# The causal convolution of a Mamba block taken into the input projection: four products per half on shifted columns

## The reference

```python
h = relu(adj @ layernorm(x) @ gcn_w + gcn_b)
h = (h - mean) * rsqrt(var + eps) * ln_g + ln_b
xz = h @ w_in                        # 128 -> 512
xc, z = xz[:, :256], xz[:, 256:]
xpad = pad(xc, 3 zero rows in front)
xconv = sum(xpad[k:k + L] * conv_w[:, k] for k in range(4)) + conv_b
u = silu(xconv)
dbc = u @ w_xp                       # 8 columns for dt, 16 for B, 16 for C
dt = softplus(dbc[:, :8] @ w_dt + b_dt)
# scan over tokens, 256 channels x 16 states:
#   state = exp(dt * A) * state + dt * B * u ;  ys = state . C
y = (ys + u * D) * silu(z)
x = x + y @ w_out
# then a mixture of 8 experts on layernorm(x): H = gelu(x @ W1 + b1), 128 -> 512,
# logits, argmax, x = x + prob * (H @ Wd[e] + bd[e])
```

## Time and profile before

| | us |
|---|---|
| median of 3 runs | 1770.6 |
| lowest, highest | 1767.5, 1779.21 |
| profiled execution, its own time | 1772.06 |
| its span (first to last instruction) | 1770.3 |
| DVE, PE, ACT, POOL busy | 1539.9, 1436.2, 883.5, 882.9 |
| mean granted TensorE clock | 0.921 |

### The profile page before, as it was taken

The page is one execution under the profiler, slowest core; times in us unless marked ns, Lnnn a source line. Parts: engine busy times, 40 slices in busy tenths (PEclk is TensorE's granted clock), DMA queues, the critical chain, the costliest instruction groups (busy, mean ns, idle before and its releaser), DMA issues. The chain is left out here.

```text
span 1770.3 us, 15687 instructions
## 1 busy us (share of the span) xinstructions
PE 1436.2 (81%) x4051; PEld 657.9 (37%) x4051; DVE 1539.9 (87%) x2038; ACT 883.5 (50%) x1574; POOL 882.9 (50%) x466
## 2 busy tenths in 40 slices
PE   6988998888888979898898888898889983522586
PEld 2433343333333434343444434343434441211343
DVE  8056989999999999999999999999999999999631
ACT  3143445453637465654747383646556473834421
POOL 0013334535346455655656564656566565656741
PEclk9999999999999999999999999999999996656698
DMA  8878999999998878788787978787887975334240
GB/s 304 279 287 274 339 343 336 348 364 354 359 331 292 299 285 304 288 292 316 266 323 263 311 266 282 278 302 276 284 318 280 324 245 171 114 115 141 86 124 12
DMA packets 151278, 476.90 MB, mean 269 GB/s; under 512 B 19694, under 2 KB 33058, under 8 KB 151060
## 3 DMA queue, kind: packets, MB, share of 16 engines
q1 hardware_dynamic: 104308, 315.57, 50.1%
q10 hardware_dynamic: 38560, 139.48, 22.9%
q0 software_dynamic: 8320, 20.86, 3.5%
HBM read 445.75 MB, written 32.97 MB: 270 GB/s over the span
## 5 line engine op out<-in xcount | busy, mean ns | idle before, releaser
L1210 PE MATMUL ps_adj<-ring,nodes 128*128 128x512 f32 x2048 | 954.4, 612 | 100.0 <-DMA ring<-adj 58.4
L499 POOL TENSOR_TENSOR h_c<-hidden,bc_ring 128x1024 f32<-128x1024 f32 x256 | 601.2, 2349 | 790.2 <-DVE inject L1070 534.6
L997 DVE TENSOR_TENSOR_SCAN hidden<-decay,state,inject 128x512 f32<-128x512 f32 x512 | 627.4, 1267 | 46.7 <-ACT decay L594 23.8
L1210 PEld LDWEIGHTS ps_adj<-ring,nodes 128*128 128x128 f32 x2048 | 389.7, 196 | 618.6 <-issue 454.2
L594 ACT ACTIVATE decay<-dt_sb,negA 128x512 f32<-128x512 f32 x512 | 339.4, 712 | 9.2 <-DVE dt_sb L1024 7.1
L1070 DVE TENSOR_TENSOR inject<-dtu_sb,bc_ring 128x1024 f32<-128x1024 f32 x256 | 314.1, 1227 | 14.5 <-DMA bc_ring<-bc_dram 12.7
L587 ACT COPY state<-hidden 128x2 f32<-128x2 f32 x255 | 49.1, 193 | 518.8 <-DVE hidden L997 518.4
L1040 DVE TENSOR_TENSOR y_sum<-y_sum,h_c 128x1024 f32<-128x1024 f32 x224 | 273.5, 1221 | 26.8 <-POOL h_c L499 23.4
L463 POOL DMA_INDIRECT out<-o_sb,out_at x68 | 100.0, 1471 | 55.7 <-DVE o_sb L900 42.5
L458 POOL DMA_INDIRECT bins<-rec,dest x60 | 87.3, 1455 | 10.8 <-issue 10.2
L453 POOL DMA_INDIRECT got<-bins,row_at x60 | 85.3, 1421 | 14.6 <-issue 11.6
(11 more groups left out here) (209 smaller groups left out, 1289.9 us busy)
## 6 DMA issues: line engine op xcount, KB each, us to landing
ring<-adj SPq DMA_DIRECT2D x512, 512.0 KB, 5.7
bc_ring<-bc_dram ACTq DMA_DIRECT2D x256, 512.0 KB, 6.4
wd_ring<-wd_rows SPq DMA_DIRECT2D x64, 288.0 KB, 5.2
bins<-nodes SPq DMA_DIRECT2D x32, 516.0 KB, 8.4
nodes<-x_rows ACTq DMA_DIRECT2D x8, 512.0 KB, 12.0
x_tile<-x_rows SPq DMA_DIRECT2D x16, 256.0 KB, 7.9
wd_rows<-Wd SPq DMA_DIRECT2D x8, 256.0 KB, 7.8
ring<-Wd SPq DMA_DIRECT2D x1, 2048.0 KB, 7.4
```

Source lines behind the costliest of these rows:

```text
L499: nc.gpsimd.tensor_tensor(h_c[:, s % 2], hidden[:, s % 2], over_halves(bc_ring[:, s % BC_RING, 1]), ALU.mult).then_inc(hc_ready, 1)
L997: scan = nc.vector.tensor_tensor_scan(hidden[:, s % 2, h], decay[:, s % 2, h], inject[:, h], state[:, h, s:s + 1], ALU.mult, ALU.add)
L1210: last = nc.tensor.matmul(ps_adj[:, 0], nodes[:, m], ring[:, g % RING, m % GROUP], start=(m == 0), stop=(m == J - 1))
```

## The change

The convolution is linear, so it goes into the projection. For each half h and tap k there is a weight win_taps[k, h] = w_in (half h) x ln_g x conv_w[:, k] (per output column). The normalised tile goes to a new buffer `hn_sb` with the last three columns of the tile before in front, and PE adds four products, each on hn_sb shifted by k columns, into one bank per half. ACT then makes u = SiLU(bank + bias) in one instruction per half. `conv_in`, the first tap on ACT and the three taps on DVE are gone. z's products now come first (f[5]) and are evicted in f[6]; the taps of half 0 stand in f[6], those of half 1 in f[7]. The fourth W1 product of the FFN moves from slot 7 to slot 8, behind the product for dbc, and the order of the GELUs follows. The counts of adjacency groups in the slots change (`SHARE`, for i from 4 on, and `MAIN[-1]`).

New at the start: the rows of conv_w are spread over the partitions by a product of the mean matrix (1/128 everywhere) with eight diagonals (times 128), on PE in the middle of tile 0's adjacency product (`tap_rows`), and multiplied with w_in and ln_g by DVE. The bias has four columns per half: in the very first tile the first three tokens see fewer taps, so they have their own (three one-column SiLUs per half in body -1).

```diff
-SHARE = (3, 3, 2, 3, 2, 2, 2, 1, 2, 2, 0, 3, 2, 3, 0, 2)
-MAIN = {-2: EVEN, -1: (0, 1, 1, 0, 0, 1, 0, 0, 5, 1, 0, 1, 1, 1, 1, 0),
+SHARE = (3, 3, 2, 3, 3, 2, 1, 0, 2, 2, 2, 3, 2, 3, 0, 1)
+MAIN = {-2: EVEN, -1: (0, 1, 1, 0, 0, 1, 0, 0, 1, 1, 0, 2, 2, 2, 2, 0),
...
-        conv_in = sb("conv_in", [P, 2, TAPS - 1 + T])
+        hn_sb = sb("hn_sb", [P, TAPS - 1 + T])
...
+        win_raw = H[:, 1].rearrange("p (k c) -> p k c", k=4)
+        diagonals = H[:, 2:4]
...
                     if front and s == f[3]:
+                        if i >= 0:
+                            c.wait(xz_done, 1, 0)
+                            nc.scalar.copy(hn_sb[:, 0:TAPS - 1], hn_sb[:, T:]).then_inc(tail_ready, 1)
                         c.wait(var_done, 1, 1)
...
                     if front and s == f[6]:
-                        c.wait(conv_step, 1, 0)
-                        nc.scalar.copy(conv_in[:, :, 0:TAPS - 1], conv_in[:, :, T:T + TAPS - 1]
-                                       ).then_inc(tail_ready, 1)
-                        c.wait(tail_ready, 1, 1)
+                        c.wait(y_ready, -1, 1)
                         for h in range(2):
                             c.wait(xz_done, 1, h + 1)
-                            nc.scalar.activation(conv_in[:, h, TAPS - 1:], ps_f[:, h], ACT.Identity,
-                                                 bias=xz_bias[:, h:h + 1]).then_inc(xz_ready, 1)
-                    if front and s == f[7]:
-
-                        c.wait(y_step, 0, 1)
-                        for h in range(2):
-                            c.wait(xz_ready, 1, h + 1)
-                            nc.scalar.activation(u_sb[:, h], conv_in[:, h, 0:T], ACT.Identity,
-                                                 bias=vec("conv_b", h), scale=vec("conv_w", TAPS * h)
-                                                 ).then_inc(conv_first, 1)
-                    if front and s == f[7]:
-                        c.wait(y_ready, -1, 1)
-                        for h in range(2):
-                            c.wait(xz_done, 1, h + 3)
                             nc.scalar.activation(z_sb[:, q, h], ps_f[:, h], ACT.Identity,
                                                  bias=xz_bias[:, h + 2:h + 3]).then_inc(xz_ready, 1)
...
                     if front and s == f[8]:
-                        c.wait(conv_step, 1, 2 * (TAPS - 1))
-                        nc.scalar.activation(u_sb[:], u_sb[:], ACT.Silu).then_inc(u_ready, 1)
-                        c.wait(xz_ready, 1, 4)
+                        c.wait(y_step, 0, 1)
+                        for h in range(2):
+                            c.wait(xz_done, 1, 3 + h)
+                            if i == -1:
+                                for t in range(TAPS - 1):
+                                    nc.scalar.activation(u_sb[:, h, t:t + 1], ps_f[:, h, t:t + 1], ACT.Silu,
+                                                         bias=tap_bias[:, h, t:t + 1])
+                            first = TAPS - 1 if i == -1 else 0
+                            silu = nc.scalar.activation(u_sb[:, h, first:], ps_f[:, h, first:], ACT.Silu,
+                                                        bias=tap_bias[:, h, TAPS - 1:TAPS])
+                        silu.then_inc(u_ready, 1)
+                        c.wait(xz_ready, 1, 2)
                         nc.scalar.activation(z_sb[:, q], z_sb[:, q], ACT.Silu)
...
-                        for k in (3, 0, 1, 2):
+                        for k in range(4):
...
+            nc.vector.tensor_scalar_mul(win_z[:], win_raw[:, 2:4], vec("ln_g")).then_inc(start_v, 1)
+            for h in range(2):
+                for k in range(TAPS):
+                    diag = nc.vector.tensor_scalar(diagonals[:, h, k * P:(k + 1) * P], ident, vec("conv_w", TAPS * h + k),
+                                                   float(P), ALU.mult, ALU.mult)
...
+            dve.wait_ge(taps_done, 1)
+            for h in range(2):
+                nc.vector.scalar_tensor_tensor(
+                    out=win_taps[:, :, h], in0=win_raw[:, h].unsqueeze(1).broadcast_to([P, TAPS, P]),
+                    scalar=vec("ln_g"), in1=ps_e[:, h].rearrange("p (k c) -> p k c", k=TAPS),
+                    op0=ALU.mult, op1=ALU.mult).then_inc(taps_ready, 1)
...
                         c.wait(rstd_ready, 1, 1)
-                        nc.vector.tensor_tensor(front_a[:], ps_f[:, 0], front_b[:], ALU.mult).then_inc(hn_ready, 1)
+                        c.wait(tail_ready, 1, 0)
+                        nc.vector.tensor_tensor(hn_sb[:, TAPS - 1:], ps_f[:, 0], front_b[:], ALU.mult
+                                                ).then_inc(hn_ready, 1)
...
-                    if front and s == f[7]:
-
-                        for k in range(1, TAPS):
-                            for h in range(2):
...
-                                nc.vector.scalar_tensor_tensor(
-                                    out=u_sb[:, h], in0=conv_in[:, h, k:k + T], scalar=vec("conv_w", TAPS * h + k),
-                                    in1=u_sb[:, h], op0=ALU.mult, op1=ALU.add).then_inc(conv_step, 1)
...
+            def tap_rows():
+
+                pe.wait_ge(diag_ready, 1)
+                for h in range(2):
+                    last = product(ps_e[:, h], [(mean, diagonals[:, h])])
+                last.then_inc(taps_done, 1)
...
+                        if (tile, g) == (0, 3 * GROUPS // 4):
+                            tap_rows()
...
                     if front and s == f[5]:
                         c.wait(hn_ready, 1, 1)
-                        for k in range(2):
-                            product(ps_f[:, k], [(win_sb[:, k], front_a[:])]).then_inc(xz_done, 1)
-                    if front and s == f[6]:
-                        for k in range(2):
-                            c.wait(xz_ready, 1, k + 1)
-                            product(ps_f[:, k], [(win_sb[:, 2 + k], front_a[:])]).then_inc(xz_done, 1)
+                        for h in range(2):
+                            product(ps_f[:, h], [(win_z[:, h], hn_sb[:, TAPS - 1:])]).then_inc(xz_done, 1)
+                    if front and s in f[6:8]:
+                        h = f[6:8].index(s)
+                        c.wait(xz_ready, 1, h + 1)
+                        product(ps_f[:, h], [(win_taps[:, k, h], hn_sb[:, k:k + T]) for k in range(TAPS)]
+                                ).then_inc(xz_done, 1)
                     if ffn and s == 7:
...
-                        for k in range(4):
-                            if k == 3:
-                                c.wait(xz_ready, 1 if front else 0, 4 if front else 0)
+                        for k in range(3):
                             product(h_bank(k), [(w1_sb[:, k], xn_cols)]).then_inc(h_done, 1)
...
+                    if ffn and s == 8:
+                        product(h_bank(3), [(w1_sb[:, 3], xn_cols)]).then_inc(h_done, 1)
                     if front and s == f[9]:
                         c.wait(low_ready, 1, 1)
                         if ffn:
-                            c.wait(h_ready, -1, 1)
+                            c.wait(h_ready, -1, 4)
```

More of the change, by code:

```diff
@@ L75, in gnn_mamba_moe @@
         gcn_sb = sb("gcn_sb", [P, P])
-        win_sb = sb("win_sb", [P, 4, P])
+        win_z = sb("win_z", [P, 2, P])
+        win_taps = sb("win_taps", [P, TAPS, 2, P])
         w1_sb = sb("w1_sb", [P, 4, P])
@@ L84, in gnn_mamba_moe @@
         xz_bias = sb("xz_bias", [P, 4])
+        tap_bias = sb("tap_bias", [P, 2, TAPS])
         eps_col = sb("eps_col", [P, 1])
@@ L348, in small_weights @@
                 sp.wait_ge(pad_ready, 1)
-                for dst, src in ((vec_sb[:], vecs), (const_sb[:], consts), (gcn_sb[:], gcn_w), (win_sb[:], w_in),
+                for dst, src in ((vec_sb[:], vecs), (const_sb[:], consts), (gcn_sb[:], gcn_w), (H[:, 1], w_in.rearrange("p k c -> p (k c)")),
                                  (wxp_sb[:], w_xp), (wdt_sb[:], w_dt[0:40]), (wout_sb[:], w_out), (w1_sb[:], W1), (wg_sb[:, :, 0:EXPERTS], Wg),
@@ L789, in _ @@
             nc.vector.memset(state[:], 0.0).then_inc(start_v, 1)
-            nc.vector.memset(conv_in[:], 0.0).then_inc(start_v, 1)
+            nc.vector.memset(hn_sb[:, 0:TAPS - 1], 0.0).then_inc(start_v, 1)
             nc.vector.memset(eps_col[:], EPS).then_inc(start_v, 1)
@@ L823, in _ @@
             dve.wait_ge(start_p, 1)
-            nc.vector.tensor_scalar_mul(win_sb[:], win_sb[:], vec("ln_g")).then_inc(start_v, 1)
+            nc.vector.tensor_scalar_mul(win_z[:], win_raw[:, 2:4], vec("ln_g")).then_inc(start_v, 1)
[3 more added lines that the diff above has]
+                                                   float(P), ALU.mult, ALU.mult)
+            diag.then_inc(diag_ready, 1)
+            dve.wait_ge(start_a, 2)
+            taps = vec("conv_w", 0, 2 * TAPS).rearrange("p (h k) -> p h k", h=2)
+            for n in range(TAPS):
+                so_far = tap_bias[:, :, n - 1] if n else vec("conv_b", 0, 2)
```

(12 more changed lines are left out.)

9 lines of the change are left out of this document (3 added, 6 removed).

## The result

| | before | after |
|---|---|---|
| median, us | 1774.8 (4 runs) | 1794.4 (4 runs) |
| lowest to highest | 1767.5 to 1779.2 | 1791.3 to 1804.6 |
| profiled execution, own time | 1772.06 | 1804.58 |
| its span | 1770.3 | 1802.8 |
| mean granted clock | 0.921 | 0.930 |

The ratio is 1.0116, interval 1.0062 to 1.017: slower by 1.2%, where 1738 (0.982 of the median then shown) was forecast.

The account below looks back on a forecast made before the run. It took DVE, 96% busy in the middle, as the bound, PE next. Eleven middle bodies gave -31 us and the start -1: 1772.06 became 1740, or 1738 as median, range 1726 to 1753 (chance 0.69).

Parts of the forecast that it names:

- Off DVE, -3.97: Convolution slot on DVE: six tap instructions a tile go, taking 3.97 us off each body.
- What surfaces, +0.85: Slot 8 on DVE: y_sum waits 0.85 us for POOL's h_c, so a body with gathers gains 3.1 us.
- PE has room: Middle bodies: PE takes 5.2 us more a tile and still has 1.6 to 3.3 us of room a body.
- The half-clock stretch goes: Middle bodies: PE's half-clock stretch after its idle time, costing 1.7 us, goes with that idle time.
- slot 10 two more: PE's slot 10 holds two more adjacency groups than before; listed without a cost in us.
- I charge 0.3 us a body: Middle bodies: later fourth FFN product delays GELUs and scan 10's decay; charged 0.3 us, 0 to 2 possible.
- the start, -1: Bodies before body 4: delays and gains nearly cancel, body 4 starts 1 us earlier; bounds -12 to +8.
- 2 us of ring waits: Start, tile 1's adjacency sum: PE's added +1.7 +5.2 us shrinks by some 2 of ring waits, to some +4.5.
- C: Rival: PE becomes the metronome, its waits stay, a body takes 100.1 us against 95.8, total 1824; chance 0.06.
- B: Rival: PE takes over evenly, its waits for u and normalised rows stay, about 1770, no change; chance 0.15.
- A: Rival: the whole convolution comes off DVE, 15 bodies x 4.0 = 60 us, 1711; chance 0.10.
- scans in slots 8 to 12 waited for ACT's decay: Sign that would prove the forecast wrong, read as PE ruling through GELU; no size given.

Follow-up runs that it names:

- hybrid5: all_order with tiles 0 to 4 convolving on DVE as before the change, taps on PE from tile 5 on: ratio 0.9838 to the kernel before.
- old_share: The changed kernel with the old SHARE table of adjacency groups: ratio 1.0068 to the kernel before.
- fetch_first: The changed kernel with ACT issuing the B and C rows' fetch at the start of slots 8, 9 and 10: ratio 1.0083 to the kernel before.
- both_old: The changed kernel with old SHARE, dbc and fourth W1 product ahead of slot 8's groups, each GELU awaiting only its product: ratio 0.9928 to the kernel before.
- all_order: both_old with the B and C rows' fetch issued at the start of slots 8, 9 and 10: ratio 0.9918 to the kernel before.
- six_early: The kernel before with six repeated z products a tile only in bodies -1 to 3: ratio 1.0083 to the kernel before.
- no_taps_dve: The kernel before with the three DVE taps of both halves left out, nothing added to PE: ratio 0.9779 to the kernel before.
- six_late: The kernel before with six repeated z products a tile only from body 4 on: ratio 1.0002 to the kernel before.
- six_more: The kernel before with each of the two z products done four times, six more products a tile: ratio 1.0103 to the kernel before.
- one_tap: The changed kernel with only the last tap's product per half instead of four, all else in its new place: ratio 1.0022 to the kernel before.
- before_again: The kernel before itself, unchanged, profiled again on the same chip as three later runs: 1775.1 us.

## Why the prediction was wrong

**Right.** *Off DVE, -3.97*: slot 7 lost 3.9. *What surfaces, +0.85*: slot 8 gained 0.9, and the waits are 0.88 and 0.83. *PE has room*: it has; its u wait is gone, the clock rose from 0.95 to 0.97, and the middle of hybrid5 runs at 93.5 with all its taps on PE, the very body that was forecast. PE's busy time a body, 798.96/9 = 88.8 in after, lies under the 90.2 to 91.9 of the forecast: of 85.4 + 5.2 = 90.6 the clock gave back 1.8. The Trainium skill, cited there ("TensorE: Matmul & The Clock Gate", "What's actually happening"), says that activity releases the throttle. By that rule added products pay part of their own price, and the trace agrees, with those 1.8 us. *The half-clock stretch goes* holds in part with it (0.95 became 0.97), and in hybrid5 (0.99, 783.79/9 = 87.1) more plainly. Tile 0's sum at 78.1 (near 78) and tile 1's at 159 (near 157) are close.

**Wrong, first step: the order of slot 10.** The text lists "slot 10 two more" among the moved groups and gives it no price. Its price is 2.6 us in slot 12 and 0.6 in slot 13, all that the middle had gained. The two groups stand in front of the logit products, ACT waits for those, and every later decay is behind ACT's wait. That was the cause: the old counts bring slot 12 back to 5.88, and with one tap, at PE's old load, it stays (7.4 to 9.7). Who waits behind a moved product was asked for slot 8 and not for slot 10. Two groups are 3.4 us of products (eight records of 0.43, by the earlier trace rows), and the wait grew from nothing in the list to 37.4/9 = 4.2.

**Wrong, second step: "I charge 0.3 us a body".** The chain (fourth W1 product, GELUs, copies, decay 10) was the right one, and in the middle of after the charge is about right: slot 9 rose by 0.2. The margin was read in one body of the middle and then used for the start, where PE runs late: ACT waits 4.6 to 5.7 us there, and slot 9 of four bodies loses 5 to 7 each, 23.7 in all. Even in the middle it holds only with the new counts; with the old ones, ACT's wait is 34.6/9 = 3.8 a body and slot 9 loses 2.2 in the mean and 4.9 at most (old_share). The text gave the upper end itself, "2 if it comes 4.4 late", and then took the lower. What the chain also carries, the issue of the B and C fetch from ACT's queue, was missing. In slot 9 it changes little but the name of the releaser (fetch_first); with the rest repaired it is what holds slot 10 (both_old against all_order).

**Wrong, third step: the start, -1.** Tile 2's sum was forecast near 235 and came at 241.7; tile 4's at "+3" and came at 432.7 against 406.3, +26. The text gave back to PE 2 us of ring waits and, of the 8 idle ones, about 3.7 (4.5 + 5.2 - 6). The term was too small even without the second step: six_early says that five bodies' products alone cost 0.8%, with the old order, where the forecast had the whole start at -1. In after the two add up: PE late makes ACT late and that makes DVE late (the rows of slot 9); that DVE's late front then delays the next sums is argued and not shown. The two do not divide cleanly. With one tap, the new places at PE's old load, the start is 597.5, where no_taps_dve has 585.1; the six products add 31 us to it in their new places (628.8), 14.7 in the old ones (six_early), and with the order repaired the start is back at 603.6 (all_order). Most of the 32 us is thus what the products and the places do together, and the steps between these traces are to be read with the 5 us by which the start moves.

**The rivals.** The sign was that of C, but its mechanism isn't what happened: PE is not the metronome (six_late 1.0002; hybrid5), its waits for u went, and the bodies of the middle take 96.8 and not the 100.1 of C. B's number for the middle, no change, came out by another road. A's 4 us a body weren't to be had: with the convolution simply left out a body takes 93.4, since the gathers do surface. The section on what would prove me wrong had the right sign for it, "scans in slots 8 to 12 waited for ACT's decay", with the wrong reading in brackets: it wasn't PE's rate, it was PE's order. A case was missing: a right balance of work, lost by the place of two products in a queue.

**The version that does it** has the gain that was forecast for the change: 0.9838, where 1738 was 0.982. It has both: the repaired order (the old counts, dbc and the fourth W1 product ahead of the groups of slot 8, a wait per GELU, the early fetch), and the taps on PE only where DVE, and not the adjacency sum, is the limit. The second without the first was not run.

## What to carry to other kernels

When a change moves products among the slots of an in-order engine, price each moved group by the instruction that now stands behind it and by everything behind that one's reader on the reader's own queue, its DMA issues too; do it for every group moved and in every regime (here: start and middle), since a margin read in one body is that body's alone. Before a change is judged by throughput, put the order back and see what is left: here the order alone was worth two per cent (1.0116 to 0.9918), and the balance of work was right in the middle. And move work to another engine only in the stretch where the relieved engine is the limit; where a sum from the other engine is awaited, the same move costs.

## What the runs showed of the hardware

- The four logit products (512 columns each, 32 output rows, into different strips of one bank) show as eight MATMUL records in 1.07 us (the row at 1082.14), where eight records of full 128-row products take 3.60: four of the eight start within 0.03 us of each other and the other four 0.46 us later, so products to different column strips run beside each other.
- More work made PE's clock better. With six more products a tile the mean granted clock of the nine bodies is 0.97 (six_more, after) and 0.99 (hybrid5), against 0.95 (and one_tap, which is after without them) and 0.96 (no_taps_dve); in the earlier trace rows the half clock follows an idle stretch. In after 5.2 us of products a body raised the busy time by 88.8 - 85.4 = 3.4.
- The same kernel had medians from 1774.4 to 1791.4 from one batch of runs to the next, one per cent, as much as the effect under study; only ratios within a batch could be compared. It isn't spread over the kernel: from the last scan to the end take 117.5 us in before_again and 132.1 in no_taps_dve, and in that stretch ACT stands still 10.0 us before one GELU, with no instruction of the program as its releaser. All eight traces of the two slower batches have such a wait there, of 8.7 to 10.9 us, and none of the others. What ACT waits for isn't shown (the batches with 1775.7 and 1791.4 carry the same chip number).
